# Summing four weight blocks with accumulating DMAs instead of GpSimd additions, in a decoder layer on one core

## What is computed

```python
x = x + L0_attn_ref(layernorm(x), Wq, bq, Wk, bk, Wv, bv, Wo, M, z)
x = x + L0_xattn_ref(layernorm(x), ctx, Wq, Wk, Wv, Wo)
x = x + L0_ffn_ref(layernorm(x), router_weight, router_bias, expert_bias)
...
q_sel = sig_q[:, :, ::G, :]
num = jnp.einsum('bshd,hde->bshe', q_sel, M)
den = jnp.einsum('bshd,hd->bsh', q_sel, z)[..., None] + EPS
out_heads = jnp.repeat(num / den, G, axis=2)
output = out_heads.reshape(b, s, H * D) @ Wo.T
```

## Time and profile before

| | us |
|---|---|
| three timed runs | 750.49, 743.04, 742.65 |
| median | 743.04 |
| the profiled execution, its own time | 745.13 |
| its span, first to last instruction | 743.0 |
| granted TensorE clock, mean | 0.993 of full |

### The profile page before, as it was taken

How to read it: one execution, slowest core, us unless ns; L and a number is a source line. 1 busy time by engine, 2 the same in 40 slices (tenths; PEclk the granted TensorE clock), 3 DMA queues, 4 the chain that set the end, 5 groups by cost and what they waited for, 6 DMA issues and landing times.

```text
span 743.0 us, 10784 instructions
## 1 busy us (share of the span) xinstructions
PE 720.2 (97%) x3644; PEld 597.9 (80%) x3644; DVE 417.1 (56%) x914; ACT 352.8 (47%) x1033; POOL 44.6 (6%) x47
## 2 busy tenths in 40 slices
PE   7998899999999999999999999999999999999996
PEld 5886678888888788888888888888888888888873
DVE  2475997676312445554464455364555446567885
ACT  3443685543323545444464454364544455444641
POOL 0026620000000000000000000000000000000000
PEclk9999999999999999999999999999999999999998
DMA  9757530003333041120041110013111001001001
GB/s 337 279 157 251 184 123 1 0 9 134 113 117 126 20 158 43 44 57 15 22 160 41 48 49 14 21 34 136 42 50 49 14 21 37 15 1 47 18 30 42
DMA packets 48545, 56.83 MB, mean 76 GB/s; under 512 B 3200, under 2 KB 29824, under 8 KB 48512
## 3 DMA queue, kind: packets, MB, share of 16 engines
q1 hardware_dynamic: 43904, 48.02, 20.1%
q10 hardware_dynamic: 4608, 8.39, 3.0%
HBM read 45.91 MB, written 10.49 MB: 76 GB/s over the span
## 4 chain that ended last, share of the span: by engine, by line
PE 90%; DVE 6%; DMA 1%; ACT 1%; issue 1%; SPq 0%; POOL 0%; ACTq 0%; DVEq 0%
PE bank L683 24%; PE bank L662 23%; PE bank L497 14%; PE bank L760 7%; PE bank L630 6%; PE bank L818 6%; PE bank L796 4%; PE bank L488 2%; PE bank L525 1%; PE bank L741 1%; DVE sig L1202 1%; DMA keys_dram<-kvout 1%; PE bank L722 1%; PE bank L571 1%; DVE kvout L1186 1%
## 5 line engine op out<-in xcount | busy, mean ns | idle before, releaser
L662 PE MATMUL bank<-xnT,regA 128*128 128x512 f32 x768 | 190.5, 398 | 0.0
L683 PE MATMUL bank<-regC,oT 128*128 128x512 f32 x768 | 180.0, 390 | 1.4 <-DVE oT L1106 1.4
L683 PEld LDWEIGHTS bank<-regC,oT 128*128 128x128 f32 x768 | 143.8, 188 | 31.5 <-DVE oT L1106 1.8
L662 PEld LDWEIGHTS bank<-xnT,regA 128*128 128x128 f32 x768 | 140.1, 188 | 28.6 <-issue 0.8
L1033 ACT ACTIVATE probs<-bank,negmax 128x128 f32<-128x128 f32 x256 | 89.8, 377 | 50.1 <-DVE negmax L1321 50.1
L1106 DVE TENSOR_TENSOR oT<-bank,oT 128x512 fp32r<-128x512 f32 x64 | 44.1, 691 | 71.1 <-ACT oT L845 70.9
L845 ACT CAST pT<-bank 128x512 fp32r<-128x512 f32 x64 | 34.5, 589 | 93.1 <-PE bank L796 93.1
L863 ACT ACTIVATE qT<-bank 128x512 f32<-128x512 f32 x64 | 39.3, 614 | 74.4 <-PE bank L662 74.3
L497 PE MATMUL bank<-regC,xnT 128*128 128x512 f32 x288 | 70.7, 397 | 0.0
L760 PEld LDWEIGHTS bank<-k_ring,qT 128*128 128x128 f32 x512 | 62.0, 191 | 3.7 <-ACT qT L863 1.1
L760 PE MATMUL bank<-k_ring,qT 128*128 128x128 f32 x512 | 62.4, 275 | 0.7 <-ACT qT L863 0.7
(11 more groups left out here) (110 smaller groups left out, 802.7 us busy)
## 6 DMA issues: line engine op xcount, KB each, us to landing
raw<-in_L_attn_Wo SPq DMA_DIRECT2D x8, 1024.0 KB, 5.7
raw<-in_L_xattn_Wo SPq DMA_DIRECT2D x4, 2048.0 KB, 9.3
wq_raw<-in_L_xattn_Wq SPq DMA_DIRECT2D x16, 512.0 KB, 4.3
k_ring<-keys_dram SPq DMA_DIRECT2D x32, 128.0 KB, 2.3
v_raw<-vals_dram SPq DMA_DIRECT2D x64, 64.0 KB, 2.3
rawk<-in_L_xattn_Wv SPq DMA_DIRECT2D x4, 512.0 KB, 4.0
rawk<-in_L_xattn_Wk SPq DMA_DIRECT2D x4, 512.0 KB, 8.2
resid<-in_x SPq DMA_DIRECT2D x4, 512.0 KB, 11.2
```

Of the source, the lines that this page charges most:

```text
L662: last = nc.tensor.matmul(k_bank[:, :], wq[:, a, head, c, :], xnT[:, b, c, half * HALF:(half + 1) * HALF], start=i == 0, stop=i == 3 * KC - 1)
L683: last = nc.tensor.matmul(bank[7][:, :], oT[:, parity, a, h, :], wo[:, b, h, :], start=h == 0 and i == 0, stop=h == GH - 1 and i == 2)
```

## The change

The slot layout of `raw16` goes. The same 16 KB per partition now hold the folded weights of all eight memories, `wofold[:, m, :, :]`, 512 values each. SP loads only the first block of each memory there, eight DMAs of 256 KB in pieces of 512 bytes. The other three blocks are added to it by DMAs with `accum_op=ALU.add`, which GpSimd's queue issues, 24 in all, of 256 KB each: `add_block(m, g)`. They stand between the roots of the norm stage, four behind each of root 1 to root 6. Block 1 waits for the first load, block 2 and 3 each for the DMA before it on the same memory. Both of GpSimd's additions are gone.

```diff
-    woa_heads = attn_Wo.rearrange("(o p) (m c) -> m p o c", p=P, m=MH)
+    woa_heads = attn_Wo.rearrange("(o p) (m g c) -> m g p o c", p=P, m=MH, g=GREP)
...
-        woa_raw = raw16[:, :].rearrange("p (r o g n) -> p r o g n", r=2, o=KC, g=GREP)
+        wofold = raw16[:, :].rearrange("p (m o n) -> p m o n", m=MH, o=KC)
...
             sp.wait_ge(tr_done, TR_CTX + NT)
             for m in range(MH):
-                if m == 2:
-                    sp.wait_ge(tr_done, tr_wqa(3) + 1)
-                    sp.dma_start(bq_all, bq_heads.broadcast_to([P, MH, P])).then_inc(rows_loaded, 16)
...
-                if m >= 2:
-                    sp.wait_ge(fold_done, m - 1)
-                sp.dma_start(woa_raw[:, m % 2, :, :, :].rearrange("p o g n -> p o (g n)"),
-                             woa_heads[m]).then_inc(woa_loaded[m % 2], 16)
...
-            sp.wait_ge(fold_done, MH)
+                sp.dma_start(wofold[:, m, :, :], woa_heads[m, 0]).then_inc(woa_first[m], 16)
+            sp.wait_ge(tr_done, tr_wqa(3) + 1)
+            sp.dma_start(bq_all, bq_heads.broadcast_to([P, MH, P])).then_inc(rows_loaded, 16)
...
+            sp.wait_ge(tr_done, tr_mem(3) + 1)
+            sp.dma_start(mem[:, :, :], mem_heads[:, MH // 2:MH, :]).then_inc(mem_loaded, 16)
+
+            sp.wait_ge(tr_done, tr_mem(MH - 1) + 2)
             sp.dma_start(wo_raw, wo_rows[:, 0:GH, :]).then_inc(wo_loaded, 16)
...
+            def add_block(m, g):
+
+                if g == 1:
+                    pool.wait_ge(woa_first[m], 16)
+                else:
+                    pool.wait_ge(woa_added[m], 16 * (g - 1))
+                pool.dma_start(wofold[:, m, :, :], woa_heads[m, g], accum_op=ALU.add).then_inc(woa_added[m], 16)
+
             for t in range(NT):
                 root(t)
-
-            for m in range(MH):
-                pool.wait_ge(woa_loaded[m % 2], 16 * (m // 2 + 1))
...
-                nc.gpsimd.tensor_tensor(w[:, :, 0:2, :], w[:, :, 0:2, :], w[:, :, 2:4, :], ALU.add)\
-                    .then_inc(fold_half, 1)
...
-                nc.gpsimd.tensor_tensor(wofold[:, m % 2, :, :], w[:, :, 0, :], w[:, :, 1, :], ALU.add)\
-                    .then_inc(fold_done, 1)
+                if 1 <= t <= 6:
+                    half, g = divmod(t - 1, GREP - 1)
+                    for m in range(4 * half, 4 * half + 4):
+                        add_block(m, g + 1)
+
...
             def wo_transposes(m):
                 k = tr_mem(m) + 1
-                pe.wait_ge(fold_done, m + 1)
+                pe.wait_ge(woa_added[m], 16 * (GREP - 1))
...
-                                               wofold[:, m % 2, c, :], ident[:, :])
+                                               wofold[:, m, c, :], ident[:, :])
```

More of the change, by code:

```diff
@@ L114, in decoder_layer @@
         qb = sb("qb", [P, 4 * P], F, first)
-        wofold = sb("wofold", [P, 2, KC, P], F, first)
         wofT = sb("wofT", [P, 2, D], R, first)
@@ L180, in decoder_layer @@
         wqa_loaded = [sem(f"wqa_loaded{i}") for i in range(4)]
-        woa_loaded = [sem(f"woa_loaded{i}") for i in range(2)]
+        woa_first = [sem(f"woa_first{i}") for i in range(MH)]
+        woa_added = [sem(f"woa_added{i}") for i in range(MH)]
         expert_loaded = sem("expert_loaded")
@@ L205, in decoder_layer @@
         rden_ready = sem("rden_ready")
-        fold_half = sem("fold_half")
-        fold_done = sem("fold_done")
         y_done = sem("y_done")
@@ L345, in _ @@
             for m in range(MH):
-                if m == 2:
-                    sp.wait_ge(tr_done, tr_wqa(3) + 1)
-                    sp.dma_start(bq_all, bq_heads.broadcast_to([P, MH, P])).then_inc(rows_loaded, 16)
-                    sp.dma_start(z_all, attn_z.rearrange("(a m) n -> a m n", a=1).broadcast_to([P, MH, P]))\
-                      .then_inc(rows_loaded, 16)
-                if m >= 2:
-                    sp.wait_ge(fold_done, m - 1)
-                sp.dma_start(woa_raw[:, m % 2, :, :, :].rearrange("p o g n -> p o (g n)"),
-                             woa_heads[m]).then_inc(woa_loaded[m % 2], 16)
-                if m == 6:
-                    sp.wait_ge(tr_done, tr_mem(3) + 1)
-                    sp.dma_start(mem[:, :, :], mem_heads[:, MH // 2:MH, :]).then_inc(mem_loaded, 16)
-            sp.wait_ge(fold_done, MH)
+                sp.dma_start(wofold[:, m, :, :], woa_heads[m, 0]).then_inc(woa_first[m], 16)
+            sp.wait_ge(tr_done, tr_wqa(3) + 1)
+            sp.dma_start(bq_all, bq_heads.broadcast_to([P, MH, P])).then_inc(rows_loaded, 16)
+            sp.dma_start(z_all, attn_z.rearrange("(a m) n -> a m n", a=1).broadcast_to([P, MH, P]))\
+              .then_inc(rows_loaded, 16)
+            sp.wait_ge(tr_done, tr_mem(3) + 1)
+            sp.dma_start(mem[:, :, :], mem_heads[:, MH // 2:MH, :]).then_inc(mem_loaded, 16)
+            sp.wait_ge(tr_done, tr_mem(MH - 1) + 2)
             sp.dma_start(wo_raw, wo_rows[:, 0:GH, :]).then_inc(wo_loaded, 16)
@@ L448, in root @@
                     .then_inc(rstd_ready, 1)
+            def add_block(m, g):
[4 more added lines that the diff above has]
+                pool.dma_start(wofold[:, m, :, :], woa_heads[m, g], accum_op=ALU.add).then_inc(woa_added[m], 16)
             for t in range(NT):
                 root(t)
-            for m in range(MH):
-                pool.wait_ge(woa_loaded[m % 2], 16 * (m // 2 + 1))
-                w = woa_raw[:, m % 2, :, :, :]
-                nc.gpsimd.tensor_tensor(w[:, :, 0:2, :], w[:, :, 0:2, :], w[:, :, 2:4, :], ALU.add)\
-                    .then_inc(fold_half, 1)
-                pool.wait_ge(fold_half, m + 1)
-                if m >= 2:
-                    pool.wait_ge(tr_done, tr_mem(m - 2) + 2)
-                nc.gpsimd.tensor_tensor(wofold[:, m % 2, :, :], w[:, :, 0, :], w[:, :, 1, :], ALU.add)\
-                    .then_inc(fold_done, 1)
+                if 1 <= t <= 6:
+                    half, g = divmod(t - 1, GREP - 1)
+                    for m in range(4 * half, 4 * half + 4):
+                        add_block(m, g + 1)
             for k in range(NT, 3 * NT):
```

## The result

The changed kernel takes 765.09 us (median of four runs, 764.75 to 766.18), the kernel before 742.97 beside it. The ratio is 1.0282, with a 95% interval from 1.0255 to 1.031: 22 us slower. I had forecast 748.5, within 1% of before.

A forecast was written before the change was run, and what follows sets the result against it. TensorE, busy 720.2 of 743.0 us, was taken to bound the kernel, waiting where GpSimd's additions stop VectorE. Lateness of 24d - 17.2 less 8.24 gave +5.5 us at 1.29 per issue d: 748.5 us, range 734.5 to 770.

The forecast's parts named there:

- the forecast's sum: Whole kernel: 24d - 25.5 us, d being one issue's time on GpSimd; +5.5 us with d = 1.29.
- the period of 0.66 + 4d: Norm stage, root to root on GpSimd: four issues of d each plus 0.66 us, five such periods up to root 7.
- the cheap rival: Norm stage: issues of at most 0.75 us hide behind PE's 3.66 us; 733.8, up to 735.6 us; chance 0.15.
- The issue's cost: GpSimd in the norm stage: one DMA issue d occupies it for 1.29 us, ends kept at 0.46 and 2.40.
- The gain: Without GpSimd's additions stopping VectorE: 8.24 us back in the memory stage, 9.2 with the norm stage's 0.94.
- From root 7 to the transposes: End of norm stage: the last tile's `xn` is ready 1.2 us after root 7 starts, then PE's transposes.
- The start at 36.0: Norm stage: the first additions wait for SP's first block, estimated to land at 36.0 us.
- What costs nothing: Loads: moved bias and z rows, memories' second half, attention's `Wo` and first loads in 512-byte pieces were to cost no time.
- The rival of the transfers: Norm stage: transfers, not issues, set the pace, 7.7 us against 5.8; 758.0 us; chance 0.12.
- VectorE stopped by the issues: Norm stage: `xn` gets in only after the fourth issue, a period of 8.6 us; 762.5 us; chance 0.08.
- From 120 us on PE is busy 20.00 of 20: Kernel before: PE has no idle time in windows from 120 us; the whole case lies in 60 us of 743.
- the likeliest case: Norm stage: issues costing between 0.75 and 1.37 us set the pace; 735.6 to 750.5 us; chance 0.43.

The follow-up runs named there:

- by_block: The changed kernel with its 24 adds reordered, four per gap still, each waiting for one issued eight adds before instead of four; 754.14 us, ratio 1.0151.
- plain: The changed kernel with accum_op left out of the 24 DMAs on GpSimd's queue, same order and waits; 755.41 us.
- quarter: The changed kernel with each adding DMA cut to the first 32 of 128 columns, as many pieces of 128 bytes; 759.71 us.
- the probe: Two runs of the kernel before with DMAs added behind its last fold: 512-byte pieces singly and paired, 745.26 us; pairs of 2 KB, 512-byte, 128-byte pieces, 749.86 us.
- shift_one: The changed kernel with each group of four adds one root later, behind root 2 to root 7; 759.69 us, ratio 1.0215.

## Why the prediction was wrong, point by point

The profiled execution came out 15.6 us over the forecast's sum (21.1 against 5.5). Of these 12.3 are root 7, which is late by 10.6 of waits, 1.3 of the start and 0.4 of small gaps; 1.2 lie between root 7 and the transposes; 2.5 are the lower clock; and 0.45 more came back than I had said.

- **The step that failed is the period of 0.66 + 4d**, "the first four end at 36.0 + 4d, root 2 follows, and then come five more periods of 0.66 + 4d". It prices what the waiting instructions cost to issue and puts their waits, behind the first, at nothing. Each add of a second or third block waits for the landing of the one issued four before, 5.5 to 12.2 us after its issue. I had noted landings only against the cheap rival. In the changed kernel these waits are 10.6 us, in seven places. `by_block` shows that they are the cause: the same issues in the same gaps, only with twice the distance between an add and the one it waits for, and the waits fall to 1.1 us, root 7 comes at 70.65 and the time is 11 us less. `plain` shows the other side: with cheaper issues and no adding the waits stand.
- **The issue's cost**, the unknown on which I had put everything, came out at 1.28 us against 1.29, but by luck. I had taken it from GpSimd's addition over as many elements. `quarter` keeps 1.28 with a quarter of the elements, the probe shows 0.90 with all of them in 128 pieces, and `plain` 0.75 without the adding, so it has nothing to do with that addition's time. The 0.11 us between instructions stood on no row; the gaps without waits came out 0.1 to 0.2 us over the formula.
- **The gain** was right in mechanism and in size. Memory steps of 4.48 us (4.50 said), `sig` at 0.69, no idle PE from the third memory on, 8.69 us back against 8.24. What took 2.5 us of it away lies in front of that stage: the lower clock behind PE's idle 7.58 us. I had seen that an idle stretch was followed by the lower clock, and left it out of the sum.
- **From root 7 to the transposes** I had 1.2 us and compared the time at which `xn` is ready with the start of the transposes. Between these two lie 0.74 us, in the earlier trace rows (54.47 + 2.62 to 57.83) as in the changed kernel, and the root's row is longer by 0.5.
- **The start at 36.0** was 37.34. `shift_one` takes that wait away and one group out of root 7's way as well, so its 5.4 us are not the price of the start alone.
- **"What costs nothing"** failed for the bias and z rows, by traffic: some 4 us of waits and clock with them, in one execution.
- **The rival of the transfers** had the right direction, and its sign, GpSimd waiting for its own DMAs, is in the profile. Its 758 us and 0.12 were too low: it counted throughput, where in a chain of landings it is latency, 5.5 to 12.2 us each under load, that counts. The runs do not separate how much of the 7.2 us is queueing from this kernel's other loads; the probe gives 4.68 without any.
- **VectorE stopped by the issues** did not happen: `xn` took 0.55 to 0.64 us behind every root of the changed kernel, and 0.99 once in `by_block`. It is the root that waits for the issues in front of it.
- **"From 120 us on PE is busy 20.00 of 20"** holds for the window from 120 to 140. Behind it PE is idle for another 10 us of 603, which the change does not touch.
- The range of 734.5 to 770 held the time; the point and the likeliest case did not.

## What to carry to other kernels

Count a dependent DMA by its landing under load, not by its issue: put between an add and the next on the same buffer at least one landing's worth of other work, and let nothing urgent stand behind the wait on the same engine. Work that is moved into the gaps of an engine which looked idle has to fit the gap with everything it waits for. Here two to a gap fitted, begun behind root 2, where four did not: 737 us against 760 for four begun at the same root, and 765 for four begun one root earlier. And a transfer whose own wait hasn't moved can still take the bandwidth from one that is now waited for.

## What the runs showed of the hardware that I had not expected

- The packets of an accumulating DMA of 256 KB in 512-byte pieces take 2.5 times the time of a plain one's under the load of this kernel (2.12 against 0.84 us, summed over 16 engines), in 528 packets instead of 80. In time the difference is smaller: 4.68 against 3.62 us for one alone, and 1.40 against 1.29 for a second beside it. Larger pieces of 2 KB did not help the adding: 6.63 us a pair against 6.52.
- Its issue on GpSimd takes 1.28 to 1.31 us with 512 pieces, whether of 512 or 128 bytes, 0.90 with 128 pieces; a plain one 0.75 with 512 pieces.
- GpSimd's power over 128 x 1, 0.55 or 0.56 us in every row before, shows up to 3.04 us behind adding issues, and 0.56 to 0.57 behind the plain ones of `plain`. It ended 0.59 to 0.60 us after the last issue in front in every case of the changed kernel, so its row has to be read from its end.
